# Low-rank attention: small products in the query product's pair of banks, as half items over all eight heads, and a row product right behind weighing

## The reference

```python
x = x + 0.5 * _L0_ffn_ref(_layernorm(x), ...)      # stage a
x = x + _L0_attn_ref(_layernorm(x), ...)           # stage w, windowed attention
x = x + 0.5 * _L0_ffn_ref(_layernorm(x), ...)      # stage b
x = x + 0.5 * _L1_ffn_ref(_layernorm(x), ...)      # stage c, quantised to 6 bits
x = x + _L1_attn_ref(_layernorm(x), ...)           # stage m
x = x + 0.5 * _L1_ffn_ref(_layernorm(x), ...)      # stage d

def _L1_attn_ref(h_t, ...):                        # 8 heads, 32 latent + 32 rotary columns
    c_q = h_t @ W_DQ + b_DQ
    c_kv = h_t @ W_DKV + b_DKV
    q = concat(c_q @ W_UQ + b_UQ, c_q @ W_QR + b_QR)
    k = concat(c_kv @ W_UK + b_UK, h_t @ W_KR + b_KR)
    attn = softmax(q @ k.T / sqrt(160))
    return (attn @ (c_kv @ W_UV + b_UV)) @ W_O + b_O

def _L1_ffn_ref(x, weight, bias):
    xq, xs = _mx_quantize(x)                       # blocks of 32, nearest 6-bit value
    wq, ws = _mx_quantize(weight)
    return (xq * xs) @ (wq * ws).T + bias
```

## Time and profile before

| | |
|---|---|
| median of three runs | 1764.55 us (1761.39 to 1765.56) |
| the profiled execution | 1760.61 us, of which its span is 1757.4 us |
| TensorE (PE) busy | 1570.5 us, 89% of the span |
| VectorE (DVE) busy | 1281.2 us, 73% |
| ScalarE (ACT) busy | 1054.1 us, 60% |
| GpSimd (POOL) busy | 1016.5 us, 58% |
| chain that ended last | PE 29%, DVE 20%; row maxima L1880 19%, weighing L1994 13% |

### The profile page before, as it was taken

The page is one execution under the profiler, slowest core; times in us unless marked ns, Lnnn a source line. Parts: engine busy times, 40 slices in busy tenths (PEclk is TensorE's granted clock), DMA queues, the critical chain, the costliest instruction groups (busy, mean ns, idle before and its releaser), DMA issues.

```text
span 1757.4 us, 42514 instructions
## 1 busy us (share of the span) xinstructions
PE 1570.5 (89%) x16971; PEld 1079.2 (61%) x16971; DVE 1281.2 (73%) x2345; ACT 1054.1 (60%) x1670; POOL 1016.5 (58%) x727
## 2 busy tenths in 40 slices
PE   4679999999877899998998999999899899999995
PEld 4557777777775555665665665566566566556554
DVE  5647777777598587786786877787787678687862
ACT  5447777777677266566555646565655655565662
POOL 5300011110056297787877788777887787777782
PEclk9879999999988599999999999999999999999998
DMA  4566656666000000000001001001001000100101
GB/s 127 126 147 153 168 145 157 156 159 155 3 28 1 1 8 11 8 11 8 11 8 22 8 11 20 8 10 20 10 8 23 7 9 10 20 10 10 21 11 31
DMA packets 198681, 81.63 MB, mean 46 GB/s; under 512 B 152552, under 2 KB 177492, under 8 KB 198356
## 3 DMA queue, kind: packets, MB, share of 16 engines
q1 hardware_dynamic: 198484, 78.93, 20.1%
HBM read 39.79 MB, written 29.88 MB: 40 GB/s over the span
## 4 chain that ended last, share of the span: by engine, by line
PE 29%; DVE 20%; issue 11%; POOL 5%; ACT 2%; SPq 0%; DMA 0%; DVEq 0%; POOLq 0%; ACTq 0%
DVE amax L1880 19%; PE pair L1994 13%; PE pair L1988 6%; PE pair L1941 3%; POOL Wm L1967 2%; PE pair L1687 2%; PE pair L1870 1%; PE pair L1729 1%; PE pair L1701 1%; PE pair L1716 1%; POOL Wm L1841 1%; POOL rstd L532 1%; ACT key_high L1755 1%; PE pair L1723 0%; PE pair L1694 0%
## 5 line engine op out<-in xcount | busy, mean ns | idle before, releaser
L1954 ACT ACTIVATE prob<-pair 128x1024 f32<-128x1024 f32 x512 | 523.2, 1025 | 338.3 <-PE pair L1941 298.0
L1880 DVE TENSOR_REDUCE amax<-pair 128x2 f32<-128x1024 f32 x512 | 585.6, 1216 | 62.5 <-PE pair L1870 61.4
L1967 POOL TENSOR_TENSOR w_mix<-w_mix,prob 128x1024 f32<-128x1024 f32 x128 | 305.1, 2384 | 74.0 <-ACT prob L1954 66.3
L1967 POOL TENSOR_TENSOR Wm<-Wm,prob 128x1024 f32<-128x1024 f32 x124 | 295.7, 2385 | 34.3 <-ACT prob L1954 27.1
L1870 PE MATMUL pair<-key_high,q_hi 64*128 64x512 f32 x1024 | 223.8, 449 | 40.7 <-DVE amax L1880 25.7
L530 POOL TENSOR_SCALAR veps<-mv 128x8 f32<-128x8 f32 x47 | 11.4, 243 | 418.0 <-DVE mv L503 416.1
L1994 PE MATMUL pair<-prob,values 128*32 128x256 f32 x4096 | 237.9, 384 | 0.0
L1196 DVE TENSOR_REDUCE mx_neg<-pair 128x4 f32<-128x512 f32 x256 | 164.7, 686 | 90.2 <-PE pair L1100 89.5
L1941 PE MATMUL pair<-q_hi,key_low 64*128 64x512 f32 x1024 | 204.3, 393 | 0.0
L1870 PEld LDWEIGHTS pair<-key_high,q_hi 64*128 64x128 f32 x1024 | 99.2, 189 | 159.1 <-DVE amax L1880 111.3
L1994 PEld LDWEIGHTS pair<-prob,values 128*32 128x32 f32 x4096 | 139.7, 112 | 88.1 <-issue 5.4
(11 more groups left out here) (229 smaller groups left out, 2628.6 us busy)
## 6 DMA issues: line engine op xcount, KB each, us to landing
rows_mem<-once SPq DMA_DIRECT2D x128, 128.0 KB, 2.0
queries<-rows_mem SPq DMA_DIRECT2D x64, 256.0 KB, 4.5
keys<-rows_mem SPq DMA_DIRECT2D x16, 1024.0 KB, 7.0
rows_mem<-once SPq DMA_DIRECT2D x128, 64.0 KB, 1.9
q_shift<-shift_cols SPq DMA_DIRECT2D x512, 0.5 KB, 2.0
yT<-o_norm SPq DMA_DIRECT2D x256, 32.0 KB, 1.8
x<-x_dram SPq DMA_DIRECT2D x8, 512.0 KB, 7.3
out_dram<-x SPq DMA_DIRECT2D x7, 512.0 KB, 3.4
```

What stands on the lines that cost most here:

```text
L1880: e.tensor_reduce(amax1[:, u % 2].rearrange("p (s t) k -> p s t k", s=2)[:, :, t, half], pair[places_m["row", r][0]][:, :].rearrange("p (s ...
L1954: e.activation(prob1[:, g % P_BUFS, :], pair[g % 2][:, :], ACT.Exp, scale=SCALE1).then_inc(*key_exp.up(g))
L1967: e.tensor_tensor(into, into, p, ALU.add).then_inc(*summed_keys.up(g))
```

## The change

The plan gives out the pairs otherwise, and the engines walk through a burst in another order. Query product and items are now one use of a pair: the query product takes bank 0 of it, the first half item bank 1, and the second half item bank 0 again, once VectorE has the low half of the query. TensorE's burst is query product, first half item, totals, second half item, weighing, row product. There is one row product in each of the eight steps. The items lie otherwise: proj is spread over heads 1 and 2, turn stays in head 3 and quant in head 0, low is spread over heads 4 and 5 together with the halves of product, and const, value and the halves of diff over heads 6 and 7. On ScalarE the items come ahead of the normalisation work. VectorE takes the first half item ahead of the work, the second between the inverse of the totals and normalising. The work of stage d moves: its statistics and its aggregate one head later, and its eight tiles at once in head 5. SyncE stores a finished batch five heads later.

```diff
-NORM_WORK = (("m stats", None), ("m aggregate", None), ("m tiles", "d stats"), (None, "d aggregate"),
-             (None, "d first tiles"), (None, "d last tiles"), (None, "d scales"), (None, "d rounding"))
-def rows_at(g):
-    r = g + ROW_LEAD
-    return {BURST: [], BURST + 1: [r - 1, r]}.get(g % NT, [r])
+EARLY_ROWS = ()
+NORM_WORK = (("m stats", None), ("m aggregate", None), ("m tiles", None), (None, "d stats"),
+             (None, "d aggregate"), (None, "d tiles"), (None, "d scales"), (None, "d rounding"))
...
-        kind, a = {0: ("quant", b - 2), 1: ("proj", b - 1), 2: ("product", b - 2), 3: ("turn", b + 1),
-                   4: ("low", b + 1), 5: ("diff", b + 1), 6: ("value", b + 1)}.get(h, (None, 0))
+        items = {0: (("quant", b - 2, 0), ("quant", b - 2, 1)), 1: (("proj", b - 1, 0),), 2: (("proj", b - 1, 1),),
+                 3: (("turn", b + 1, 0), ("turn", b + 1, 1)), 4: (("low", b + 1, 0), ("product", b - 2, 0)),
+                 5: (("low", b + 1, 1), ("product", b - 2, 1)), 6: (("const", b + 1, 0), ("diff", b + 1, 0)),
+                 7: (("value", b + 1, 0), ("diff", b + 1, 1))}[h]
...
-        rows = [r for r in rows_at(g) if 0 <= r < NT * U]
+        row = g + ROW_LEAD if 0 <= g + ROW_LEAD < NT * U else None
...
-        for r in rows:
-            use(("row", r), [("row", r, 0)])
...
-        if query is not None:
-            use(("query", query), [("query", query, 0)])
+        if query is not None or items:
+            use(("items", g), ([("query", query, 0)] if query is not None else []) + items)
         if weigh is not None:
             use(("weigh", weigh), [("weigh", weigh, 0)])
-        if items:
-            use(("items", g), items)
+        if row is not None:
+            use(("row", row), [("row", row, 0)])
...
+        def item_bank(g, n):
+            return 2 * places_m["items", g][0] + 1 - n
...
         def pe_low_rank(e):
...
-                for r in rows:
-                    pe_row_scores(e, r)
+                if query is not None or items:
+                    pair_free(e, ("items", g))
                 if query is not None:
-                    pair_free(e, ("query", query))
-                    pe_low_part(e, ("query", query, 0), 2 * places_m["query", query][0])
+                    pe_low_part(e, ("query", query, 0), item_bank(g, 1))
+                for n, item in enumerate(items[:1]):
+                    pe_low_part(e, item, item_bank(g, n))
+                if weigh is not None:
+                    pe_totals(e, weigh)
+                for n, item in enumerate(items[1:], start=1):
+                    if query is not None:
+                        low_bank_free(e, ("query", query, 0))
+                    pe_low_part(e, item, item_bank(g, n))
+                if row is not None and early_row(g):
+                    pe_row_scores(e, row)
                 if weigh is not None:
                     pe_weigh(e, weigh)
-                if items:
-                    pair_free(e, ("items", g))
-                for n, item in enumerate(items):
-                    pe_low_part(e, item, 2 * places_m["items", g][0] + n)
+                if row is not None and not early_row(g):
+                    pe_row_scores(e, row)
...
         def act_low_rank(e):
...
-                for kind, b in work:
-                    act_norm_work(e, kind, b)
...
                 for item in copies:
                     act_low_after(e, item)
                 for n, item in enumerate(items):
-                    act_low_part(e, item, 2 * places_m["items", g][0] + n)
+                    act_low_part(e, item, item_bank(g, n))
+                for kind, b in work:
+                    act_norm_work(e, kind, b)
...
         def dve_low_rank(e):
...
-                for r in rows:
-                    dve_row_max(e, r)
-                    if r % NT == NT - 1:
-                        dve_row_top(e, r // NT)
                 if query is not None:
-                    dve_low_part(e, ("query", query, 0), 2 * places_m["query", query][0])
+                    dve_low_part(e, ("query", query, 0), item_bank(g, 1))
+                for n, item in enumerate(items[:1]):
+                    dve_low_part(e, item, item_bank(g, n))
                 for kind, b in work:
                     dve_norm_work(e, kind, b)
                 if weigh is not None:
                     dve_invert_totals(e, weigh)
+                for n, item in enumerate(items[1:], start=1):
+                    dve_low_part(e, item, item_bank(g, n))
...
+                if weigh is not None:
                     dve_normalise(e, weigh)
-                for n, item in enumerate(items):
-                    dve_low_part(e, item, 2 * places_m["items", g][0] + n)
+                if row is not None and not early_row(g):
+                    dve_row_max(e, row)
+                    if row % NT == NT - 1:
+                        dve_row_top(e, row // NT)
...
-                if h == 3 and 2 <= b < B:
-                    sync_store(e, b - 2)
+                if h == 0 and 3 <= b <= B:
+                    sync_store(e, b - 3)
```

50 lines of the change are left out of this document (26 added, 24 removed).

## The result

The changed kernel takes 1689.32 us (median of four runs, 1686.91 to 1693.71), where the kernel before took 1765.05 beside it (1761.39 to 1769.46): a ratio of 0.957, with an interval of 0.954 to 0.960. That is 75.7 us less. The prediction said 93.3 less, 1671.3. The profiled execution took 1689.08 us, 71.5 less than the profiled one of before.

A forecast was written before the change was run, and what follows sets the result against it. Each head was a chain: TensorE from query to first maximum, VectorE's maxima to the next query. Savings of 8.8 + 84.5 = 93.3 us took the median from 1764.55 to 1671.3 us, range 1655 to 1686 (chance 0.63).

The forecast's parts named there:

- Plain head, 14.69 us: Head without small products: row product behind weighing brings the first maximum 0.69 us earlier, 15.38 to 14.69 us.
- First half item, -0.38 for each head with one: Between query product and totals on TensorE: a half item fills some 0.38 us of waiting.
- rival A: Exponentials set the pace between first maximum and query, costing 0.3 to 0.5 us a head: 1691 to 1701, chance 0.17.
- Second half item, TensorE's time of before and 0.06 of waiting: Between totals and weighing: TensorE's time unchanged, 0.06 us of waiting in heads 0 and 3, none elsewhere.
- Head 6, 17.3 us because the scale waits for GpSimd: VectorE's queue in head 6: the scale waits for GpSimd's sum, 17.3 us; without the wait 16.3.
- Head 4's waiting goes: Early turn product lets GpSimd's sums end before head 4's totals; their 2.56 us wait, slow weighing and late evacuation go.
- other moves, nothing: Moved d tiles, later store, row products ahead of step 0: hidden, worth nothing, with 1 us either way.
- Tail and opening at nothing: Outside the loop: no rows left to gain by in the tail; row products placed otherwise ahead of step 0 worth nothing.
- The signs named: Query to first maximum 8.7 us (head 7), 8.1 (head 4); head 4's totals wait under 0.3; eight maxima 9.14.
- B: TensorE's clock still falls twice a batch, behind const and value for one; 16 times 1.5 us return: 1695, chance 0.12.
- C: The halves cost what they save; only head 4's waiting goes, 5.5 us in seven batches: 1726, chance 0.04.
- D: Slower: GpSimd's sums come late in most heads, 3.9 us per wait; 1913 if in all 62, chance 0.03.

The follow-up runs named there:

- the new table: Kernel before with only the work on d moved (statistics and aggregate one head later, eight tiles in head 5): 1737.1 us, ratio 0.987.
- the old table: Changed kernel with the work on d back in its earlier heads (statistics head 2, aggregate head 3, tiles heads 4 and 5): 1684.24 us, ratio 0.956.

## Why the prediction was right or wrong

The direction and the range held, and so did the main savings: the row product's place, the cover for the half items, the end of the stall. The size was 18 us too large in the median, and one piece of the chain was wrong: what paces the query. Step by step:

- **Plain head, 14.69 us: measured 14.69 to 14.71, by two errors that cancel.** "From there to the next query, paced by the maxima" failed. The maxima pace the next totals, 9.2 us from the first one, and the query is paced by key scores and exponentials: 8.26 us became 8.49. In a plain head the totals lose a wait of 0.2 us for that, so the sum is right by luck.
- **First half item, -0.38 for each head with one: 0.18.** With the rows as before it does give 0.38: head 4 of the second batch is 15.99 us, and 15.99 - 15.39 = 0.60 for a half item of 0.99. But the row's bracket shows only 0.19 us of waiting, and that is the wait that the earlier row product takes away too. The prediction counted it twice. The other 0.2 is not waiting: ahead of the totals low costs 0.80 us (they start at 1.52 instead of 0.72), where 0.99 was its price behind weighing. In the changed kernel that head takes 15.51 us, 0.81 above the plain one. So the two together are worth 0.68 + 0.38 - 0.2. That is 0.2 us in 49 heads (those with an item, head 6 apart), about 10 of the 16 us missing in the loop. It is rival A in a mild form: the sign that I had named was a stretch above 8.5 us, and 8.48 to 8.49 stay just short of it.
- **Second half item, TensorE's time of before and 0.06 of waiting: 0.1 to 0.2 us more.** In head 4 weighing starts 4.04 us behind the query with the product between, and 2.84 in the second batch, which has none: 1.20 where 1.0 was the price. The 30 heads with a second half item, head 6 apart, exceed the prediction by that much beyond the 0.2 above, some 6 us in all, the rest of the 16. It is not the wait for the low half of the query, which ends 0.5 us before the product starts (1067.70, 1068.21).
- **Head 6, 17.3 us because the scale waits for GpSimd: 17.1 to 17.4 in five of six batches.** In the second batch, where the scale met only the last 0.1 us of the sum, it is 16.64. The mechanism was right, shown by taking the scale away from VectorE: 16.35.
- **Head 4's waiting goes: it does.** In the kernel before the new table takes away 3.8 to 4.1 us a head in five batches and 3.0 in one, where the clock fell behind a later wait. The reason given was half of it. I had read GpSimd's wait for the features (3.4 us) as the cause; the aggregate behind it (2.7) was needed as well, and its move alone gives the 24.6 us. The place of the d work was put under "other moves, nothing". It was worth the whole stall in the kernel before, and in the changed kernel it costs 3.3 us: with the old table GpSimd is ahead in head 6, and the scale takes 0.56 us there instead of 1.69.
- **Tail and opening at nothing.** The tail is 2.4 us longer, 0.8 of it from the quant half between totals and weighing, the rest mostly slower projections, which some runs of the same order don't show. The 3.5 us by which the stage started later are no part of the change, and its first two query products lay anywhere from 21.5 to 24.6 us apart in these kernels; from the stage's first query product to the start of the loop it was 1.3 us more. So the span fell by 77.3 - 2.4 - 3.5 - 1.3 = 70.1 us, and the profiled execution by 71.5.
- **A slip in the sum.** The second batch was put at 128.4 us. It lacks the quant item and both product halves, which by the prediction's own prices makes 127.3. The 52 heads also end behind five heads of the last batch, not four. The two nearly cancel: 840.9 in place of 841.3.
- **The signs named.** The first maximum of head 7 came at 8.81 us (8.7 said), of head 4 at 8.25 (8.1). The totals of head 4 wait for nothing, and eight maxima take 9.15. Weighing in head 4 starts at 4.04, below 2.3 plus its items, so no second item waits for VectorE by that sign either.

What the second half item costs beyond its price lies where TensorE goes from 32 columns of its array to the whole and back, and the weight loads show it. In head 2 of the third batch, where nothing stands between totals and weighing, weighing's loads start 0.21 us ahead of its first matmul (904.39):

```profile
904.18 3.37 PEld L1984 LDWEIGHTS pair<-prob,values 128*32 128x32 f32 x64
```

With the product between, in head 4 of the fourth batch, its loads stand still for 0.41 us and then begin together with its first matmul, and those of weighing begin together with theirs as well (1069.30):

```profile
1068.21 0.97 PEld L1690 LDWEIGHTS pair<-up_gated,yT 128*128 128x128 f32 x8 [0.41 <-issue]
```

The row product ahead of weighing paid the same (0.55 us in place of 0.34). No run takes the change of columns away alone, so this is the likely cause, not a shown one.

Of the rivals, B (the clock falls behind narrow products) is out for the changed kernel: 1.00 in all heads of the loop. Its suspicion was right for the kernel before, where the falls in head 6 cost 0.8 to 1.1 us each in four batches, 3.8 us in all, and are part of what the change gains; the prediction gave no reason why they should go. C (only head 4 goes) is out: 52.7 of the 77.3 us come from elsewhere. D is out: the totals waited for a sum once in the loop, 0.19 us.

The 77.3 us of the loop come to 24.6 for the stall, 24.4 for the row product as it is worth beside the rest, and by subtraction 28.3 for all else: the halves ahead of the totals, out of the way of the first maximum, spread over eight heads, and the 3.8 us of clock. No run has the halves alone, so this last share is argued and not measured.

## What to carry to other kernels

When two engines share buffers in turn, ask of each wait which buffer ends it, not which stretch it seems to fill: the maxima were found at the right pace and hung on the wrong product, and two savings that both draw on one wait were added. Price pairs of edits together if each removes a wait of the same product. When an engine comes late, list everything between its wait and the work that is due; a short stall and a few small steps may be harmless each alone, and then the cheaper of two remedies will do.

## What the runs showed of the hardware

A VectorE instruction of 32 elements per partition took 1.69 us when it met a sum by GpSimd, and ended within 0.05 us of it, in two forms: two scalars on one tile, and one scalar with two tiles. How long the first form took depended on when in the sum it began: 2.24 us from 0.16 us into it (last batch of the changed kernel), 0.56 from 1.87 into it (old table), each time ending with the sum; and 0.18 us where it began 0.01 us ahead of the sum (head 6 of the second batch, rows as before). By that the 0.70 us of the earlier trace rows was a wait too. A reciprocal of the same tile ran through another such sum in its usual 0.35 us. The Trainium skill (SBUF — State Buffer, section "Who interferes with whom") says that a VectorE instruction with two inputs in SBUF, the on-chip memory that holds the tiles, contends with a GpSimd instruction that reads it, and that the form with scalars can too; both runs agree with it. I had taken the second form as a way round.

TensorE's granted clock fell from the upper of its two levels (2.4 GHz) to the lower (1.2 GHz) for 3.4 us at a time in the loop of the kernel before. In head 4 this came each time TensorE had stood some 2.6 us ahead of the totals (a mean of 0.92 to 0.93 in that head), and it was gone in five of six batches once the d work was moved and the wait with it. In head 6 it came right behind the const and value products, in four of six batches with the stall and in four of six without it (a mean of 0.91, 19.0 us against 18.2); key scores took 0.64 us a pair in it instead of 0.39. In the changed kernel, where const and value stand in two heads, it came in none of the 60 heads. That standing or narrow products bring the fall is suggested by what came before each, not shown: in two of the six batches the same products in head 6 were followed by none, and of seven heads 4 with the wait of 1.76 us one had a fall behind it.
